# Arccos attention with an expert layer: TensorE's value sums for a batch's last four tiles are issued one at a time between the next batch's cosines

## What is computed

```python
qkv = x @ w_qkv.T + b_qkv
q = _l2norm(to_heads(q))
k = _l2norm(to_heads(k))
cos = jnp.einsum('bhsd,bhtd->bhst', q, k)
g_dist = jnp.arccos(jnp.clip(cos, -1.0 + EPS, 1.0 - EPS)) * SPHERE_RADIUS
attn_score = (1.0 + g_dist / BANDWIDTH ** 0.5) ** (-D_INTRINSIC - ALPHA)
n_r = jnp.sum(attn_score, axis=-1)
n_c = jnp.sum(attn_score, axis=-2)
k_tilde = (n_r ** (-A))[..., :, None] * attn_score * (n_c ** (-A))[..., None, :]
probs = k_tilde / jnp.maximum(jnp.sum(k_tilde, axis=-1, keepdims=True), 1e-12)
out = jnp.einsum('bhst,bhtd->bhsd', probs, v)
```

## Time and profile before

| | |
|---|---|
| median of 3 runs | 5208.56 us (5207.46 to 5214.79) |
| the profiled execution's own time | 5210.09 us |
| its span in the trace | 5208.4 us |
| ACT busy | 4836.7 us, 93% |
| DVE busy | 4099.7 us, 79% |
| PE busy | 3098.4 us, 59% |
| POOL busy | 1830.9 us, 35% |
| mean granted TensorE clock | 0.748 of full speed |

### The profile page before, as it was taken

The page is one execution under the profiler, slowest core; times in us unless marked ns, Lnnn a source line. Parts: engine busy times, 40 slices in busy tenths (PEclk is TensorE's granted clock), DMA queues, the critical chain, the costliest instruction groups (busy, mean ns, idle before and its releaser), DMA issues.

```text
span 5208.4 us, 37394 instructions
## 1 busy us (share of the span) xinstructions
PE 3098.4 (59%) x10654; PEld 799.6 (15%) x10654; DVE 4099.7 (79%) x4051; ACT 4836.7 (93%) x1280; POOL 1830.9 (35%) x565
## 2 busy tenths in 40 slices
PE   8655546544554456455546666565656565665799
PEld 4200001000100000000011111111111111111244
DVE  7777878778787777877878888788878888888577
ACT  5899999999999999999999999999999999999621
POOL 0324443344433444334424443344324432444000
PEclk9856786677667766766677778687877878687799
DMA  2200000000000000000000101010100101010200
GB/s 90 65 10 12 19 18 14 12 17 18 18 14 16 13 10 10 9 3 10 12 30 24 37 27 37 5 50 10 36 26 24 36 22 38 5 53 2 82 31 14
DMA packets 71908, 127.84 MB, mean 25 GB/s; under 512 B 9735, under 2 KB 47254, under 8 KB 71767
## 3 DMA queue, kind: packets, MB, share of 16 engines
q1 hardware_dynamic: 70615, 122.17, 7.5%
q0 software_dynamic: 1152, 4.19, 0.3%
HBM read 96.33 MB, written 29.88 MB: 24 GB/s over the span
## 4 chain that ended last, share of the span: by engine, by line
ACT 56%; issue 22%; DVE 11%; PE 7%; DVEq 1%; DMA 0%; SPq 0%; ACTq 0%
ACT X L1306 14%; ACT X L1279 13%; ACT X L1290 10%; ACT X L1298 9%; ACT X L1319 7%; DVE X L1067 4%; PE psum L1535 3%; DVE ncol L1075 3%; ACT L1290 1%; DVE rows L1172 1%; PE psum L934 1%; DVE X L1053 1%; PE psum L949 1%; PE psum L908 1%; PE psum L1500 0%
## 5 line engine op out<-in xcount | busy, mean ns | idle before, releaser
L1252 POOL TENSOR_TENSOR X<-X 128x2048 f32<-128x2048 f32 x504 | 1797.9, 3601 | 2817.6 <-DVE X L1053 2817.6
L908 PE MATMUL psum<-stacks 128*128 128x512 bf16 x4096 | 1653.6, 497 | 829.8 <-DVE X L1067 438.3
L1067 DVE TENSOR_TENSOR X<-psum,X 128x1024 f32<-128x1024 f32 x1024 | 1190.3, 1217 | 421.3 <-ACT X L1290 384.8
L934 PE MATMUL psum<-X,vp 128*32 128x512 f32 x4096 | 697.3, 843 | 1152.5 <-DVE vp L1081 1152.5
L1075 DVE TENSOR_REDUCE ncol<-X 128x4 f32<-128x8192 f32 x126 | 1094.0, 8682 | 364.3 <-ACT X L1319 359.1
L1053 DVE TENSOR_SCALAR X<-psum 128x1024 f32<-128x1024 f32 x1024 | 1189.7, 1216 | 31.4 <-DVE rows L1172 25.1
L1298 ACT ACTIVATE X<-X 128x4096 f32<-128x4096 f32 (+1 forms) x192 | 898.0, 4739 | 22.9 <-DVE X L1067 22.9
L1290 ACT ACTIVATE X<-X 128x4096 f32<-128x4096 f32 x256 | 904.8, 3605 | 0.7
L1306 ACT ACTIVATE X<-X,consts 128x16384 f32<-128x16384 f32 x64 | 892.9, 13951 | 0.8
L1279 ACT ACTIVATE X<-X,consts 128x8192 f32<-128x8192 f32 x126 | 889.7, 7108 | 0.0
L1319 ACT ACTIVATE X<-X 128x8192 f32<-128x8192 f32 x126 | 878.9, 7022 | 2.0
(11 more groups left out here) (176 smaller groups left out, 1157.3 us busy)
## 6 DMA issues: line engine op xcount, KB each, us to landing
V<-expert_w SPq DMA_DIRECT2D x64, 512.0 KB, 3.6
stacks<-qk_parts SPq DMA_DIRECT2D x256, 64.0 KB
qk_parts<-X SPq DMA_DIRECT2D x96, 128.0 KB, 1.9
stacks<-qk_parts SPq DMA_DIRECT2D x64, 192.0 KB
head_out<-evac SPq DMA_DIRECT2D x32, 256.0 KB, 2.1
expert_w<-u_t SPq DMA_DIRECT2D x17, 256.0 KB, 2.6
X<-in_L_attn_x_dram POOLq DMA_DIRECT2D x8, 512.0 KB, 4.3
stacks<-qk_parts SPq DMA_DIRECT2D x32, 128.0 KB
```

Of the source, the lines that this page charges most:

```text
L908: return nc.tensor.matmul(dst, stacks[:, 1, buf, keys:keys + P], stacks[:, 0, buf, q0:q0 + n], start=True, stop=True)
L934: mm = nc.tensor.matmul(ps_sum[32 * j:32 * j + 32, :], vp[:, i, :], X[:, m % 2, i, j * 512:(j + 1) * 512], start=(m % 2 == 0 and i == 0), ...
L1067: nc.vector.tensor_tensor(part, ps_cos[j % 2], part, ALU.mult).then_inc(cos_ok, 1)
L1252: nc.gpsimd.tensor_tensor(own, own, own, ALU.mult).then_inc(square_ok, 1)
```

## The change

In TensorE's `emit` the adds of tiles 0 to 3 stay as they were. The adds of tiles 4 to 7 are no longer issued together: after each of them the cosines of one tile of the next batch's `mult` (tiles 1 to 4) are issued; tiles 5 to 7 follow. No instruction is added, dropped or changed in shape; no other engine's order is touched. Where there is no next batch, the order is as before.

```diff
                     if has(k, m + 1):
                         mult(k, m + 1, 0)
-                    for i in range(BT):
+                    for i in range(BT // 2):
                         add(k, m, i)
+
+                    for i in range(BT // 2, BT):
+                        add(k, m, i)
+                        if has(k, m + 1):
+                            mult(k, m + 1, i - BT // 2 + 1)
                     if has(k, m + 1):
-                        for i in range(1, BT):
+                        for i in range(BT // 2 + 1, BT):
                             mult(k, m + 1, i)
                     if has(k, m + 2):
                         clip(k, m + 2, 0)
```

## The result

The change is slower: 5232.89 us median (5 runs, 5229.64 to 5234.44) against 5211.16 us for the kernel before (5 runs). The ratio is 1.0039, 95% interval 1.0029 to 1.0050. That is 0.4% in place of the forecast "no difference"; it lies inside the range I gave and on the side of rival 1.

A forecast was written before the change was run, and what follows sets the result against it. ScalarE's chain was taken to bound the attention. Quiet batches +15.6 us and late ones -20.1 gave net -4.5, from 5210.1 to 5205.6, stated as 5205 us; range 5188 to 5240.

The forecast's parts named there:

- no difference: Whole kernel: 5205 us, within the 10.4 us (about 0.2%) a measurement can tell from no change; chance 0.50.
- rival 1: Clock stays low through interleaved cosines of tiles 2 and 3: 5294 us never rising, 5244 one add later; chance 0.28.
- 11 late batches: Batches where VectorE's expert sums delay `vp` and the arctangent waits; predicted to wait 2.8 us in place of 22.9, -20.1.
- 52 quiet ones: Batches whose adds were hidden and whose arctangent did not wait; predicted to pay 0.3 us each, +15.6 us.
- the chain itself: Cosines and adds from tile 0's first product to tile 3: 1.7 us per batch at the lower clock, nothing at the upper.
- VectorE's lateness: Rival cause of the late batches' wait: they keep it, only +15.6 is left, 5226 us; chance 0.02.
- I take 0.3 us per batch: ScalarE's wait per quiet batch: mean 0.23 us over the clock's rises, plus allowance for the unknown switch and small gap.
- I let the rise come evenly between 2.7 and 5.8 us into the chain: When TensorE's clock goes up among the interleaved adds and cosines, range taken from add blocks of 4.94 to 6.40 us.
- half of an unknown 0.1: Switch from cosines to adds on TensorE: no measured row, bounded by 0 and 0.1 us per add, middle taken.
- the slack: Time between VectorE finishing tile 3 and ScalarE's arctangent starting: 0.9 us in a quiet batch, 1.0 in a late one.
- The formula with its allowance: Rise at x: ScalarE waits x/2 - 1.95 us, nothing to 3.9, 0.5 from 4.9 to 5.8; plus switch and small gap.
- the 22.9 us: The arctangent L1298's wait for VectorE's products, in 11 batches before the change; the most the change could remove.

The follow-up runs named there:

- run 3: The change plus 18 matmuls with unused results behind the add of tile 4, in the attention's first half only: 5213.94 us.
- run 2: The change's order only for batches behind m = 3 and m = 0 of the side work, the order before in all others: 5197.25 us.
- run 4: The change plus one small ScalarE copy per batch, result unused: 5235.54 us.
- run 5: The kernel before plus one small ScalarE copy per batch, result unused: 5226.91 us.

## Why the prediction was wrong

**Right.** That ScalarE's chain bounds the attention and L1298's wait is the place where the change acts; that 11 late batches gain and 52 quiet ones pay; the chain itself, its order of events and the place of the wait, ahead of tile 2 with a little more ahead of tile 3; that the lower level of the clock makes the cost (run 3) and the adds, not VectorE's lateness, the old wait (run 2); the waits of at most about 1 us, and VectorE's wait for L908 growing, though to 92.0 and not to about 60. L1298's own waits were put at about 18 us in all and came to 33.9.

**Wrong.** The step that failed is "I take 0.3 us per batch", with "I let the rise come evenly between 2.7 and 5.8 us into the chain" behind it. The quiet batches of the first half pay 0.73 us each. Two things are in it:

- *The switches between adds and cosines at the lower level were priced too low.* I had 0.1 us from adds to cosines, taken at the upper level, and half of an unknown 0.1 for the other way. The weight loads of the quiet batch after the change, timeline of PEld, show both at the lower level:

```profile
2058.86 0.13 PEld L908 LDWEIGHTS psum<-stacks 128*128 128x128 bf16 x2 [1.00 <-DVE X L1072]
2059.82 0.20 PEld L934 LDWEIGHTS psum<-X,vp 128*32 128x32 f32 x8 [0.84 <-issue]
2061.69 0.13 PEld L908 LDWEIGHTS psum<-stacks 128*128 128x128 bf16 x2 [1.66 <-DVE X L1072]
2062.10 0.15 PEld L908 LDWEIGHTS psum<-stacks 128*128 128x128 bf16 x1 [0.28 <-issue]
2062.52 0.15 PEld L908 LDWEIGHTS psum<-stacks 128*128 128x128 bf16 x1 [0.28 <-issue]
```

  From two cosines to the add 0.96 us passed, where 0.87 were reckoned, and from the add to the next cosine 1.87 where 1.71 were due: about 0.1 and 0.16, together 0.26 per add in place of 0.15. The Trainium skill's rule quoted in the prediction ("TensorE: Matmul & The Clock Gate", section "The mechanism") had both switches costing. The trace shows both costs, 0.1 and 0.16 us, but not that the rule is their reason: the last two rows are loads of cosines behind cosines, on all rows as well, and they come 0.42 us apart, where one of the two matmuls that take 0.87 us is due 0.43, so there a load costs nothing.

  The wait of VectorE at tile 2 is 1.61 us, where the chain had 1.4. By the length of the batches a rise 3.5 us into the chain cost ScalarE 0.1 us and one at 5.5 cost 0.76 (run 4, over the 72.96 us of run 5); one at 4.2 cost 0.40 and one at 6.3 cost 1.05 (the change, over 72.66). The prediction's chain gives nothing for 3.5, 0.5 for 5.5, 0.17 for 4.2 and, carried on beyond its range, 0.64 for 6.3. For the two places of the change that is 0.4 in the mean, or nearly 0.5 with the 0.07 added for the unknown switch and the small gap, where 0.73 was paid. That is the first part, about 0.25 us per batch. Most of it is the switches; a little is the slack, which comes out of these waits at 0.87 and 0.78 us in place of 0.9.
- *The rises are neither spread evenly nor within the range.* In the kernel before, where TensorE's clock changed nothing for ScalarE, the batches drift past the clock's changes. With the change the rise came 4.2 and 6.3 us into the chain in turn in the first half, and the later of the two lies beyond the 5.8 that I had as the end. The formula with its allowance gives nearly 0.5 us for these two places and 0.3 for the even spread. That is the second part, about 0.18 us per batch. I read it so: as soon as a late rise makes a batch longer, the next batch meets the clock at another place, and the two settle. Runs 4 and 5 bear this out: the copy that cost 0.31 us per batch in the first half of the kernel before cost 0.01 there in the change (0.3 us in 33 batches); the rises kept their 146.77 us and the waits shrank.

With 0.73 us for the first half's 33 batches, 0.5 for the second half's 18 quiet ones and 0.7 (7.5/11) for the late ones in place of 0.25, the sum comes to +24.2 + 9.1 - 16.7 = +16.6 us against the -4.5 forecast. The number of batches and the 22.9 us were right, and the slack nearly. (5205.6 less 1.5 is 5204.1 and not the 5205 of the forecast, which matters to nothing.) Rival 1 had the sign and the cause, and its price for a late rise, a mean wait of 0.9 us and +34, is nearer to what happened than the forecast; but the clock did not stay down: in the first half it rose within each chain, only later than the slack allows.

## What to carry to other kernels

Before moving work from an engine's idle time to between operations that another engine is waiting for, look at which of those operations the bounding engine needs first, and put the work behind them: here two tiles further down turned +0.4% into -0.4%. Look up in the trace at which level of the clock TensorE's work behind an idle time runs (here the lower one, behind 7.43 us), and price it at that level, switches of operand shape included. And where a wait depends on when the clock rises, do not average over its place: a loop with such a wait can fall into step with the clock, as this one did, and then pays the same waits again and again.

## What the runs showed that I had not expected

- The loop's period and TensorE's clock fall into step. Without a wait on the clock every batch of the first half took 72.65 or 72.66 us; with it, batches alternate between 73.06 and 73.71 us (one copy added: the same), or go through 74.02, 74.40 and 73.45 us in turn (two copies). Adding 0.31 us of ScalarE work per batch cost 0.3 us in 33 batches; adding a second copy of the same size brought that to 17.8 us.
- Useless matmuls paid: 18 per batch in the first half brought 19 us against the change, by holding the clock at its upper level into the chain in most batches; that only made up for the change (1.0004 of the kernel before).
- TensorE's busy time fell with the change, from 3098.4 to 2867.6 us, and its mean clock rose from 0.748 to 0.784, while the kernel became slower. Once the clock had risen in the interleaved stretch it stayed up through the cosines that follow, as at 2063.90 to 2072.00; before, those had run at 0.50 for 27.30 us. Neither figure told the time here: ScalarE sets it, and its waits grew from 22.9 to 33.9 us.
